# The plan's float32 K in the Sinkhorn attention: read back from a ring in DRAM, or summed again from its halves

## The reference, cut to what matters

```python
def _sot(q):
    qn = q / (norm(q) + 1e-08)
    C = 1.0 - einsum('bhnd,bhmd->bhnm', qn, qn)
    C = where(eye, 1000.0, C)
    log_K = -C / 0.1
    log_v = zeros
    for _ in range(10):
        log_u = log_marg - logsumexp(log_K + log_v[..., None, :], -1)
        log_v = log_marg - logsumexp(log_K + log_u[..., :, None], -2)
    z = exp(log_u[..., :, None] + log_K + log_v[..., None, :])
    z = z / max(z, axis=(-2, -1))
    return where(eye, 1.0, z)
attn = softmax(_sot(q) * 16 ** -0.5)
out = attn @ v
```

## Time and profile before

| | |
|---|---|
| median of 3 runs | 4972.74 us (4967.56 to 4984.73) |
| the profiled execution | 4981.01 us |
| its span | 4979.2 us, 192120 instructions |
| PE busy | 4554.7 us (91%) |
| PEld busy | 3664.8 us (74%) |
| DVE busy | 3720.6 us (75%) |
| ACT busy | 3105.1 us (62%) |
| DMA | 232.97 MB, mean 47 GB/s |

### The profile page before, as it was taken

How to read it: one execution, slowest core, us unless ns; L and a number is a source line. 1 busy time by engine, 2 the same in 40 slices (tenths; PEclk the granted TensorE clock), 3 DMA queues, 4 the chain that set the end, 5 groups by cost and what they waited for, 6 DMA issues and landing times. The chain is left out here.

```text
span 4979.2 us, 192120 instructions
## 1 busy us (share of the span) xinstructions
PE 4554.7 (91%) x84693; PEld 3664.8 (74%) x84710; DVE 3720.6 (75%) x8486; ACT 3105.1 (62%) x4620; POOL 313.2 (6%) x347
## 2 busy tenths in 40 slices
PE   5999999976899999999999999999999879599992
PEld 3777777742688888888888888888888745277771
DVE  8999999944488888887888888877777746355556
ACT  4777777722566666666666666666666325377776
POOL 0000000000000000000000000000000005523331
PEclk9999999986899999999999999999999979699996
DMA  1010000023001111111121112100000024322224
GB/s 64 28 36 33 27 27 27 17 93 82 25 17 32 29 34 32 30 28 23 37 46 37 39 42 49 30 23 16 17 16 15 6 90 159 130 65 69 68 69 163
DMA packets 190201, 232.97 MB, mean 47 GB/s; under 512 B 81024, under 2 KB 159104, under 8 KB 187328
## 3 DMA queue, kind: packets, MB, share of 16 engines
q1 hardware_dynamic: 175872, 189.76, 14.2%
q0 software_dynamic: 13632, 32.66, 1.8%
HBM read 144.09 MB, written 78.25 MB: 45 GB/s over the span
## 5 line engine op out<-in xcount | busy, mean ns | idle before, releaser
L699 PE MATMUL y_ps<-k_sb,x_sb 128*12 128x256 f16 x58368 | 1693.0, 273 | 36.4 <-DVE x_sb L960 28.3
L699 PEld LDWEIGHTS y_ps<-k_sb,x_sb 128*12 128x12 bf16 x58368 | 1458.7, 88 | 174.3 <-DVE x_sb L960 37.5
L831 ACT ACTIVATE y_sb<-y_ps 128x256 f32<-128x256 f32 x912 | 347.5, 381 | 778.9 <-PE y_ps L699 778.8
L840 ACT ACTIVATE k_new<-cos,k_bias 128x512 f32<-128x512 f32 x768 | 520.4, 682 | 171.5 <-PE cos L726 171.5
L709 PEld LDWEIGHTS turned_x<-rows_in,y_sb 128*128 128x128 f32 x3648 | 471.8, 192 | 99.6 <-issue 52.8
L991 DVE CUSTOM_DVE_ANT_0 plan<-plan,u_rows,v_last 128x512 f32<-128x512 f32 x768 | 535.1, 744 | 4.1
L257 PE MATMUL acc<-w_hl,feat_h 128*128 128x384 f16 x2688 | 455.6, 327 | 87.5 <-ACT feat_h L242 87.5
L709 PE MATMUL turned_x<-rows_in,y_sb 128*128 128x16 f32 x3648 | 511.4, 257 | 9.1 <-ACT y_sb L831 8.2
L1006 DVE TENSOR_TENSOR k_sb<-k_new,k_sb 128x2048 f16<-128x2048 f32 x192 | 439.3, 2288 | 65.9 <-ACT k_sb L848 61.9
L854 ACT ACTIVATE plan<-plan,p_bias,p_scale 128x1024 f32<-128x1024 f32 x384 | 464.4, 1237 | 9.6 <-DVE p_scale L1002 9.6
L979 DVE TENSOR_TENSOR plan<-k_sb 128x1024 f32<-128x1024 f16 x384 | 459.2, 1217 | 0.0
(11 more groups left out here) (261 smaller groups left out, 7226.1 us busy)
## 6 DMA issues: line engine op xcount, KB each, us to landing
x_in_sb<-expert_rows SPq DMA_DIRECT2D x39, 528.0 KB
xt<-in_x_dram SPq DMA_DIRECT2D x16, 1280.0 KB, 6.0
q_left<-q_parts SPq DMA_DIRECT2D x192, 64.0 KB, 3.9
q_right<-q_parts SPq DMA_DIRECT2D x192, 64.0 KB, 4.0
raw<-in_w_dram SPq DMA_DIRECT2D x24, 384.0 KB, 4.2
w<-w_halves SPq DMA_DIRECT2D x16, 576.0 KB, 7.3
w<-expert_results SPq DMA_DIRECT2D x24, 384.0 KB, 6.7
v_parts<-v_sb SPq DMA_DIRECT2D x16, 408.0 KB, 2.4
```

Source lines behind the costliest of these rows:

```text
L699: last = nc.tensor.matmul(y[a][32 * c:32 * c + XW, :, :], high[:, j, XW * h:XW * (h + 1)], k_sb[s][:, h, :, at:at + P], start=(h == 0 and ...
L831: nc.scalar.activation(y_sb[a][:, :, :], y[a][:, :, :], ACT.Copy).then_inc(rows_read[a], 1)
L840: nc.scalar.activation(k_new[h % 2][:, c, :], cos[:, c % 2, :], ACT.Exp, bias=k_bias[:, 0:1], scale=1.0 / (REG * Q_SCALE ** 2), accum_out= ...
```

## The change

The float32 K of each head is stored to DRAM as it is built and loaded again before the plan needs it. `k_all` is a ring of RING = 5 groups, 4 heads, 4 pieces of 128 x 512 float32 (256 KB, contiguous in DRAM). SP stores a piece as soon as its exponent is done (`store_k`, one or two pieces a cycle) and loads two pieces in eight of the ten cycles (`load_k`, by LOADS_OLD for heads 2 and 3 of group G - 2 and LOADS_NEW for heads 0 and 1 of group G - 1), that is three to five cycles before their `times_u`. SP's queue now walks through the cycles, with a wait for TensorE's turn of the young group at each. `plan` has four buffers in place of two. `join` and its counter are gone; `times_u` waits for `k_in[h]`, the first exponents of a head wait for `k_out[h % 2]` (the stores of the head before it in that `k_new` buffer), and `high_parts` has no wait for `joined`. The store of the attention rows moves to cycle 4. The counters of `project` are handed to `attend` and cleared by SP at its start.

```diff
--- before
+++ after
@@ constants @@
+RING = 5
+LOADS_OLD = {0: (2, (0, 1)), 1: (2, (2, 3)), 3: (3, (0, 1)), 4: (3, (2, 3))}
+LOADS_NEW = {6: (0, (0, 1)), 7: (0, (2, 3)), 8: (1, (0, 1)), 9: (1, (2, 3))}
@@ attend, buffers and counters @@
-        plan = two("plan", [P, TB, TOKENS], F32)
+        plan = [sb(f"plan{h}", [P, TB, TOKENS], F32) for h in range(GH)]
...
-        joined, u_rows_ready, plan_ready, head_max_ready = (
-            sem("joined"), sem("u_rows_ready"), sem("plan_ready"), sem("head_max_ready"))
+        u_rows_ready, plan_ready, head_max_ready = sem("u_rows_ready"), sem("plan_ready"), sem("head_max_ready")
+        k_out, k_in = [sem(f"k_out{a}") for a in range(2)], [sem(f"k_in{h}") for h in range(GH)]
@@ attend, sync @@
+            def store_k(G, h, chunks):
+                H = (G + 1) * GH + h
+                for c in chunks:
+                    after(sp, k_exp, H * TB + c + 1)
+                    sp.dma_start(k_all[(G + 1) % RING, h, c, :, :], k_new[h % 2][:, c, :]).then_inc(k_out[h % 2], 16)
+
+            def load_k(F, h, chunks):
+                if chunks[0] == 0:
+                    after(sp, pv_ready, (F - 1) * GH + h + 1)
+                    after(sp, k_out[h % 2], 16 * TB * ((F * GH + h) // 2 + 1))
+                for c in chunks:
+                    sp.dma_start(plan[h][:, c, :], k_all[F % RING, h, c, :, :]).then_inc(k_in[h], 16)
...
-                if tail:
-                    after(sp, att_ready, (G - 2) * GH)
-                    store(t - 1, s)
-
+                for i in range(CYCLES):
+                    f, c = i // 5, i % 5
+                    a, b = 2 * f, 2 * f + 1
+                    if young and i > 0:
+                        after(sp, turned[0], G * YOUNG + i - 1)
+                    if i in LOADS_OLD and fin:
+                        load_k(G - 2, *LOADS_OLD[i])
+                    if i in LOADS_NEW and old:
+                        load_k(G - 1, *LOADS_NEW[i])
+                    if i == 4 and tail:
+                        after(sp, att_ready, (G - 2) * GH)
+                        store(t - 1, s)
+                    if build:
+                        store_k(G, *((a, (0, 1)), (a, (2, 3)), (b, (0, 1)), (b, (2,)), (b, (3,)))[c])
+
+            for counter in over:
+                sp.sem_clear(counter)
             sp.wait_ge(zeroed, START + ZEROS)
             phases(sp, phase)
...
+                sp.wait_ge(k_out[a], START + 16 * TB * ALL_GROUPS * GH // 2)
@@ attend, tensor: times_v; scalar: weights; vector: times_u @@
-  plan[h % 2]
+  plan[h]
@@ attend, scalar: exponents @@
                     if c == 0:
                         after(act, k_built, H - 1)
+                        after(act, k_out[h % 2], 16 * TB * (H // 2))
@@ attend, scalar: high_parts @@
-                if fin:
-                    after(act, joined, (G - 2) * GH + h + 1)
@@ attend, vector @@
-            def join(F, s, h, half):
-                H = F * GH + h
-                if half == 0:
-                    after(dve, pv_ready, H - 1)
-                cols = slice(half * 2 * TOKENS, (half + 1) * 2 * TOKENS)
-                done = nc.vector.tensor_tensor(plan[h % 2][:, 2 * half:2 * half + 2, :].rearrange("p b n -> p (b n)"),
-                                               k_sb[s][:, h, 0, cols], k_sb[s][:, h, 1, cols], ALU.add)
-                if half == 1:
-                    done.then_inc(joined, 1)
...
             def times_u(F, s, h, chunks):
                 H = F * GH + h
                 if chunks[0] == 0:
-                    after(dve, joined, H + 1)
+                    after(dve, k_in[h], 16 * TB * (F + 1))
@@ attend, vector: phase @@
-                            join(G - 2, new, a, 0)
-                            join(G - 2, new, a, 1)
                             times_u(G - 2, new, a, (0, 1))
                     if c == 1 and fin:
                         times_u(G - 2, new, a, (2, 3))
-                        join(G - 2, new, b, 0)
                     if c == 2:
                         if build:
                             low_parts(G, new, a)
-                        if fin:
-                            join(G - 2, new, b, 1)
@@ tower @@
+    k_all = scratch("k_all", (RING, GH, TB, P, TOKENS), F32)
...
-        project(nc, h, wqv, ident, q_parts, v_parts)
+        over = project(nc, h, wqv, ident, q_parts, v_parts)
```

More of the change, by code:

```diff
@@ L479, in _ @@
             images(dve, nothing, split, read_low)
+    return counters
 GH = 4
@@ L501, in after, with attend @@
         eng.wait_ge(counter, START + count)
-def attend(nc, q_parts, v_parts, ident, pick_rows, att, w, w_halves, unscale):
+def attend(nc, q_parts, v_parts, k_all, ident, pick_rows, att, w, w_halves, unscale, over):
     with ExitStack() as ctx:
@@ L759, in times_v @@
                         last = nc.tensor.matmul(pv[32 * c:32 * c + HD + 1, 0:P], v_sb[s][:, j, h, :],
-                                                plan[h % 2][:, j, c * P:(c + 1) * P], start=(j == 0), stop=(j == TB - 1))
+                                                plan[h][:, j, c * P:(c + 1) * P], start=(j == 0), stop=(j == TB - 1))
                 last.then_inc(pv_ready, 1)
@@ L841, in exponents, with high_parts @@
                                          scale=1.0 / (REG * Q_SCALE ** 2), accum_out=row_sums[s][:, c, h:h + 1]).then_inc(k_exp, 1)
-            def high_parts(G, s, h, fin):
+            def high_parts(G, s, h):
                 H = (G + 1) * GH + h
                 after(act, k_exp, (H + 1) * TB)
-                if fin:
-                    after(act, joined, (G - 2) * GH + h + 1)
                 nc.scalar.activation(k_sb[s][:, h, 0, :], k_new[h % 2][:, :, :].rearrange("p b n -> p (b n)"), ACT.Copy).then_inc(k_high, 1)
@@ L852, in weights @@
                     after(act, scale_ready, F * GH + h + 1)
-                part = plan[h % 2][:, 2 * half:2 * half + 2, :]
+                part = plan[h][:, 2 * half:2 * half + 2, :]
                 nc.scalar.activation(part, part, ACT.Exp, bias=p_bias[:, 0:1], scale=p_scale[h % 2][:, 0:1]).then_inc(p_ready, 1)
@@ L901, in phase @@
                         exponents(G, new, a, (2, 3))
-                        high_parts(G, new, a, fin)
+                        high_parts(G, new, a)
                     if c == 2 and build:
@@ L913, in phase @@
                         if build:
-                            high_parts(G, new, b, fin)
+                            high_parts(G, new, b)
             phases(act, phase)
@@ L990, in times_u @@
                 for c in chunks:
-                    last = nc.vector.tensor_tensor_reduce(plan[h % 2][:, c, :], plan[h % 2][:, c, :], u_rows[:, :],
+                    last = nc.vector.tensor_tensor_reduce(plan[h][:, c, :], plan[h][:, c, :], u_rows[:, :],
                                                           v_last[s][:, c, h:h + 1], 0.0, ALU.mult, ALU.max, row_max[:, c:c + 1])
@@ L1977, in tower @@
         clear(nc, embed(nc, x, freqs, w_tok, h))
-        project(nc, h, wqv, ident, q_parts, v_parts)
+        over = project(nc, h, wqv, ident, q_parts, v_parts)
         unscale = ctx.enter_context(nc.sbuf_tensor("unscale4", [P, 2], F32))
-        attend(nc, q_parts, v_parts, ident, pick_rows, att, mix_w, halves, unscale)
+        attend(nc, q_parts, v_parts, k_all, ident, pick_rows, att, mix_w, halves, unscale, over)
         mix(nc, h, att, ident, mix_w, halves, unscale, soft_rows_out, soft_results_out)
```

## The result

| | before | after |
|---|---|---|
| median of 7 runs | 4977.92 us (4967.56 to 4987.86) | 5015.5 us (4996.94 to 5027.73) |
| the profiled execution, its span | 4981.01, 4979.2 us | 5020.46, 5018.7 us |
| DVE busy | 3720.6 us | 3295.8 us |
| DMA | 232.97 MB, 47 GB/s | 635.80 MB, 127 GB/s |

What follows compares the result with a forecast made beforehand. The prediction took TensorE, busy 55.2 us a phase, as the attention stage's bound. Its terms, -6 + 20 + 2 + 7 = +23 us, gave 4996 us on the median's scale, with a range of 4955 to 5085.

Steps and rivals of the forecast that it cites:

- Relief at nothing: At phase ends, removing the Vector engine's sums of halves would not shorten TensorE's waits for x: gain 0.
- Rival C: At phase ends, Vector relief removes the 15.2 us of waits and idle around weight loads: 4948 us; chance 0.10.
- The tail, -6: In the last finishing phase and the one before, removing sums ahead of products with u saves 6 us.
- Latency and the new waits at 0: K pieces return with two cycles of margin, 11 us against 3.5; new Scalar and SP queue waits cost 0.
- Rival E: Some K arrives late at a use, a microsecond or more per late head: 5100 us and more; chance under 0.02.
- Floor of 55.2: In attention phases TensorE is always busy for 55.2 us, a floor no relief of the Vector engine lowers.
- the SBUF contention at nothing: In the attention stage, added transfers would not slow the Vector engine through SBUF: cost 0.
- one stall of 1.0 us in each: At starts of the 28 phases with weight pieces, longer bunches delay program fetches: 28 less 7.9, +20 us.
- rival D: Stalls past 1.5 us in 28 phases lower TensorE's clock, 5.5 us each: +154, 5120 us; chance 0.05.
- The other cycles and phases, +2 and +7: Bunches starting the 18 phases without weight pieces cost +2 us; the other eight cycles of 46 phases, +7 us.
- rival B: Bunches in all ten cycles of 46 phases stall TensorE 0.11 to 0.3 us each: 5017 to 5110 us; chance 0.17.
- Rival A: Program fetches keep their margin because contiguous K pieces drain fast; only the 6 us gain remains: 4967 us; chance 0.30.

Runs made afterwards that it cites:

- Run 1: Changed kernel without the K stores and loads and the waits on them, no sums, plan buffers holding ones: 4977.3 us, ratio 1.0001 to the kernel before.
- run 3: Changed kernel with the weight pieces' loads and half stores moved from the phase's start to other cycles, same transfers: 4969.91 us, ratio 0.9989.
- run 2: Changed kernel with the 384 sums of halves still made, into a buffer nobody reads: 5015.19 us, ratio 1.008.
- run 6: Kernel before, sums kept, with only the weight piece's Vector work put ahead of the low parts of K: 4957.14 us, ratio 0.9962.
- run 8: Changed kernel with weight pieces spread, plus two 384 KB loads of contiguous rows at each start of phases 20 to 33: 4996.04 us, ratio 1.0032.
- runs 10: Changed kernel with the K stores but no K loads, the plan's K made by the sums of halves: 4981.5 us, ratio 1.0006.
- 11: Changed kernel without K stores, sums kept, with as many 256 KB loads from another tensor into unread buffers: 5012.65 us, ratio 1.0059.
- runs 5: Changed kernel with weight pieces spread over the cycles and their Vector work ahead of the low parts of K: 4953.03 us, ratio 0.9946.
- 9: Changed kernel with weight pieces spread, their Vector work ahead of the low parts of K, and q and v spread too: 4956.39 us, ratio 0.9951.
- 7: Kernel before, sums kept, with weight pieces spread and their Vector work ahead of the low parts of K: 4947.05 us, ratio 0.9935.
- run 4: Changed kernel with the weight piece's maximum and low half put ahead of the low parts of K on the Vector engine: 4983.84 us, ratio 1.0012.

## Why the prediction was right, and where its sizes were off

**The direction and the mechanism** held: 4996 forecast, 5015.5 measured (+23 forecast, +38 found), by late program blocks at the starts of the phases with weight pieces (39 of the 40 waits on issue end within 20 us of the first load of q). Run 1 ties all of it to the transfers, run 3 to their bunching, and the landings of the blocks to the waits.

**Relief at nothing:** right. The wait for x stayed at 0.5 to 0.6 us a phase; it was 17.3 us without sums (run 1), 17.1 with them (run 2) and 2.0 with them in run 6, so the sums never held it. Rival C is out.

**The tail, -6:** it measured -5.1.

**Latency and the new waits at 0:** right. Stores land in 2.9 us and loads in 3.5 in the median (2.5 and 3.5 assumed; 5.5 and 6.5 in the bunch above), and neither the Scalar engine's wait on k_out nor the Vector engine's on k_in shows in the trace. Rival E is out. **Floor of 55.2:** right (55.25). So is the SBUF contention at nothing: the Vector engine's plan instruction took 744 ns in both kernels, its low parts of K 2288 ns before and 2289 after.

**The term that was mis-sized:** "one stall of 1.0 us in each" of the 28 phases with weight pieces, +20. The 27 whole phases of the windows cost 8.0 + 32.0 = +40 us. I priced both stretches alike, and they aren't: the 14 phases of the first cost 0.6 us more each, which is less than I took, and the 13 of the second 2.5 us. In the first only one weight piece goes with q and v at a phase's start, in the second two do, behind the halves; run 8 says that two loads are enough. There one bunch gave two stalls, as in the timeline above, single ones grew to 3.4 us, and behind three of over 2 us the clock fell. That last part is rival D in three phases instead of 28, and its price of 4 us beyond a wait was about right. I had taken the mean and the longest wait of the bunches of before for the ends of this term; a bunch half as long again went beyond both. The length was also not the whole measure: by runs 10 and 11 the same bytes cost nothing measurable as stores and 0.59% as loads, and the prediction priced both alike.

**The other cycles and phases, +2 and +7:** together about +5 of the stage, so small, as taken; rival B is out, with 55.25 us in clean phases at a share of 0.52. Sum of what was found: -5.1 + 40 + 5 = +40, against 39.5 between the two spans. The forecast had about half of the main term; the wide range, not the sum, held the time.

**Rival A** was wrong for this bunch and nearly right elsewhere. K's contiguous pieces cost some 6 to 9 us, at the edge of the noise, once no weight pieces lie ahead of them (runs 5 and 9 against 7). Its reason, the pitch of the weights, is out by run 8.

**What stays open:** that the waits on issue are waits for late blocks is shown by when the blocks land. How the data traffic delays a block, and why loads do it more than stores, is not; no run delayed the program's queue by itself.

## What to carry to other kernels

Before work is traded for transfers, ask which wait it ends: 467 us of an engine that nobody waited for were worth 5 us, while two instructions exchanged ahead of a wait were worth 19 (run 6). In an unrolled program, take waits on "issue" behind full stretches of DMA for program blocks that come late, and compare where they end with when the blocks land; spread the transfers over the cycle, loads first, and look at the share in windows of 10 us, since the average hides it. Price a stall by its tail too, because the clock may go down behind it.

## What the runs showed that I had not expected

- The direction matters: at 103 GB/s each, 768 stores of 256 KB cost 0.06% (within the noise) and 768 loads 0.59%.
- The change's worst bunch was made by transfers that it did not add: moving the weight pieces alone gave back some 45 us, more than the 38 that were lost.
- The clock didn't follow the length of a stall alone: in the change 1.79 and 1.92 us brought no fall and 2.05 us did, in the kernel before one of 1.55 us had the earlier trace rows, in run 4 one of 1.14 us did, and in run 10 one of 2.50 us did not.
